# A D1 macaron layer on one core: attention probabilities turned in 32x32 squares by VectorE and a trip through DRAM

## The chip, the cores and the metric

One core of a Trainium2 chip. The metric is the device time of the core in microseconds; lower is better. The kernel before takes 1220.16 us, the median of 3 runs (1220.13 to 1220.35).

## The reference

```python
x = x + 0.5 * ffn(layernorm(x))          # x: 2 x 512 x 512 float32
x = x + attention(layernorm(x))
x = x + 0.5 * ffn(layernorm(x))
# attention, 32 query heads, 8 key/value heads of width 128, causal with an ALiBi bias:
scores = einsum('bkgqd,bksd->bkgqs', rmsnorm(q), rmsnorm(k)) / sqrt(128)
attn = softmax(scores + bias)            # bias is -1e30 above the diagonal
out = einsum('bkgqs,bksd->bkgqd', attn, v)
return out.reshape(b, s, 32 * 128) @ Wo.T
```

The feed-forward part is a gated linear unit whose weights are scaled by a product of rank 4. Everything is float32; TensorE works in a rounded format, so each operand is kept as a high part and a rest, and each product is made of three: high by high, high by low, low by high.

## The kernel before

The work is a first feed-forward pass, the attention, and a second feed-forward pass. The attention is cut in 64 **units**, `unit(n)` being one key/value head g with its 4 query heads, one batch and one block of 128 queries: n = 8 g + 4 b + t. A unit has t + 1 key blocks. Below, i is n modulo 4 (which is t) and "at" is n modulo 8.

Each engine has a program of its own, written out by hand as `slot(n)` for n = 0 to 63. Semaphores couple them; an engine takes its instructions strictly in order.

**TensorE** (`slot`, L707), in slot n: scores of unit n (for i = 0 in halves, L655 to L657, else L367 to L369 through `matmul3`); `weigh_values(n - 1)` (L677): for each key block the values' high part and rest times the high part of the turned probabilities (L688, L689), then the values' high part times their rest (L693); two of seven products that make queries, keys and values of the two units four slots ahead (`product_qkv`); `turn_rows(n + 1)`, whose results the next scores need (L619, L622); `project_out(n - 1)`, 12 products; one or two more products of the seven; and last `turn_probabilities(n)` (L666, instruction L674): for each key block, four 128x128 transposes against an identity into one PSUM bank.

**ScalarE** (`slot`, L1105): `exponentials(n)`, in between or behind them `weigh_values(n - 1)` (high part of the weighed values, L1086), `probabilities(n)` (L1075, times the inverse sum), takes of sums out of PSUM (`take_sum`, L1023), `turn_rows(n + 1)` (L1049, L1058), high parts of the next head group's weights (`split_qkv`, L977, instruction L988), `take_left` (L1030), and `turn_probabilities(n)`, the high part of each turned block (L1081).

**VectorE** (`slot`, L1602): `scores(n)` adds the bias and finds the top (L1517; at i = 0 L1504 and L1509), then sums of squares (L1466) and inverse roots in even slots, the inverse sum (L1522), `weigh_values(n - 1)` (rest, L1541), `add_products` (L1560), `turn_rows(n + 1)` (L1484, L1494), `project_out(n - 1)` (adds into a ring of two rows, L1550), and last `turn_probabilities(n)` (L1535): the rest of each turned block.

**GpSimd** (`slot`, L1819): squares of rows (L1811), norms (`norm_rows`, L1817), rests of the values, of the output weights (`split_o`) and of the group's weights (`split_qkv`), all through L1686, and `mix_qkv` (L1747, instruction L1761), which makes mixed weight blocks t1 to t4 out of b11, b12, b21 and b22. `QKV_WHEN` says in which slot of a group which block of the next group is split: b11 and b21 at 2, t2 and t1 at 3, t3, t4 and b22 at 4. Mixes t1 to t3 are made at 3, t4 at 4. The first products that use them are issued in slot at=4. A mixed block can be rounded by ScalarE only when GpSimd has made it:

```python
if block[0] == "t":
    act.wait_ge(qkv_mixed, QKV_MIXES.index((g, block)) + 1)
```

**SP** issues all transfers of this stretch from one queue: `load_qkv(g + 1)` at 1 and `load_o(g + 1)` at 6, both into the same room, so that each waits for the splits of the other; and for each unit `ring_store`, which waits for VectorE's add, and `ring_load`, which waits for the store to land.

Probabilities (`prob`), their turned parts (`probT_h`, `probT_l`) and the weighed values (`oT_h`, `oT_l`) have one room each. TensorE rotates over 7 PSUM banks in this stretch.

## Time and profile before

| | |
|---|---|
| median of 3 runs | 1220.16 us |
| the profiled execution, first to last instruction | 1218.6 us |
| TensorE busy | 1206.2 us, 99% |
| VectorE, ScalarE, GpSimd busy | 834.9, 753.5, 652.8 us |
| granted TensorE clock | 1.000 |
| turning of probabilities on TensorE | 640 instructions |
| DMA, mean | 77 GB/s |

Busy times of TensorE are of pipelined instructions whose ends are modelled: what one costs is the distance between starts.  A row of a stretch gives, behind its length, how long each engine was busy in it, with the number of instructions in brackets.

### The profile page before, as it was taken

The page shows a single profiled execution, that of the slowest core. Times are in us where ns is not written, and L with a number is a line of the kernel's source. Part 1 is how long each engine was busy: PE and PEld are TensorE (multiplying, and loading weights), DVE is VectorE, ACT ScalarE, POOL GpSimd, SP SyncE. Part 2 cuts the span into 40 slices and gives each one's busy share as a digit, 9 for nine tenths or more (in the row PEclk, how much of TensorE's full clock was granted, in tenths as well). Part 3 has the DMA queues.
Part 4 walks back from the last instruction along what each step waited for, and adds up shares of the span by engine and source line. Part 5 has one row for each costly group of instructions (what it writes and reads, how often), then busy time and mean ns, then how long its engine had stood idle before and what let it go on. Part 6 is the DMA issues. An engine that isn't in the chain of part 4 may idle for free.

```text
span 1218.6 us, 18533 instructions
## 1 busy us (share of the span) xinstructions
PE 1206.2 (99%) x6368; PEld 1062.1 (87%) x6368; DVE 834.9 (69%) x2035; ACT 753.5 (62%) x1758; POOL 652.8 (54%) x526
## 2 busy tenths in 40 slices
PE   6999999999999999999999999999999999999999
PEld 5888888899998999999999999999999888888887
DVE  7876665776666577677677677667767878755555
ACT  4554442357677767767768767767767774544442
POOL 5796561635675625724824824823824343865550
DMA  6152222212213123122122122122122020221101
GB/s 235 42 175 94 103 105 104 94 47 87 79 44 104 44 79 103 39 84 96 44 87 89 50 87 87 53 79 96 53 78 87 20 68 9 71 69 53 52 18 69
DMA packets 33596, 93.77 MB, mean 77 GB/s; under 512 B 4128, under 2 KB 5056, under 8 KB 31456
## 3 DMA queue, kind: packets, MB, share of 16 engines
q1 hardware_dynamic: 33264, 92.29, 22.2%
q8 instruction: 52, 0.85, 0.3%
q14 instruction: 40, 0.33, 0.1%
q10 hardware_dynamic: 240, 0.30, 0.1%
HBM read 62.69 MB, written 29.88 MB: 76 GB/s over the span
## 4 chain that ended last, share of the span: by engine, by line
PE 98%; DVE 1%; DMA 0%; ACT 0%; SPq 0%; issue 0%
PE bank L369 22%; PE bank L367 22%; PE bank L368 21%; PE bank L674 6%; PE bank L479 4%; PE bank L473 4%; PE bank L474 4%; PE bank L688 3%; PE bank L693 3%; PE bank L689 3%; PE bank L619 2%; PE bank L395 1%; PE bank L655 1%; PE bank L622 1%; PE bank L383 1%; DMA x_rows<-x 0%
## 5 line engine op out<-in xcount | busy, mean ns | idle before, releaser
L1066 ACT ACTIVATE prob<-prob,neg_top 128x128 f32<-128x128 f32 (+3 forms) x256 | 141.2, 554 | 87.6 <-DVE neg_top L1517 56.9
L1817 POOL TENSOR_TENSOR rows<-rows,row_root_y 128x640 f32<-128x640 f32 x64 | 80.5, 1257 | 194.1 <-DVE row_root_y L1205 192.9
L1811 POOL TENSOR_TENSOR square<-rows 128x640 f32<-128x640 f32 x64 | 79.3, 1254 | 158.7 <-DVE rows L1560 131.1
L1686 POOL TENSOR_TENSOR w_l_late<-raw_late,w_h_late 128x512 fp32r<-128x512 f32 (+1 forms) x59 | 91.5, 1565 | 71.8 <-ACT w_h_late L809 71.8
L1075 ACT ACTIVATE prob<-prob,inverse 128x128 f32<-128x128 f32 (+3 forms) x252 | 121.1, 553 | 4.4 <-DVE inverse L1522 4.4
L1535 DVE TENSOR_TENSOR probT_l<-bank,probT_h 128x512 fp32r<-128x512 f32 x160 | 101.4, 683 | 28.5 <-ACT probT_h L1081 28.5
L1081 ACT CAST probT_h<-bank 128x512 fp32r<-128x512 f32 x160 | 84.6, 596 | 41.4 <-PE bank L674 41.4
L1281 DVE SCALAR_TENSOR_TENSOR x_rows<-bank,x_rows 128x512 f32<-128x512 f32 x111 | 74.8, 687 | 44.4 <-PE bank L479 44.4
L367 PE MATMUL bank<-o_h,oT_h 128*128 128x512 f32 x256 | 104.7, 409 | 0.0
L369 PE MATMUL bank<-o_h,oT_l 128*128 128x512 f32 x256 | 100.8, 394 | 0.0
L368 PE MATMUL bank<-o_l,oT_h 128*128 128x512 f32 x256 | 99.8, 390 | 0.0
L1517 DVE CUSTOM_DVE_ANT_0 prob<-bank,bias 128x256 f32<-128x256 f32 (+3 forms) x200 | 97.0, 540 | 0.0
L1560 DVE TENSOR_TENSOR rows<-bank,rows 128x384 f32<-128x384 f32 x72 | 40.0, 555 | 79.2 <-ACT rows L1023 51.3
L674 PE MATMUL bank<-ident,prob 128*128 128x128 f32 x640 | 80.9, 273 | 0.3 <-ACT prob L1075 0.3
L674 PEld LDWEIGHTS bank<-ident,prob 128*128 128x128 f32 x640 | 73.8, 140 | 4.9 <-issue 0.9
L1686 POOL TENSOR_TENSOR w_l_early<-raw_early,w_h_early 128x512 fp32r<-128x512 f32 x37 | 48.6, 1328 | 41.5 <-ACT w_h_early L809 41.5
L367 PE MATMUL bank<-kT,qT_h 128*128 128x256 f32 (+3 forms) x192 | 67.7, 352 | 0.0
L841 ACT COPY part<-bank 128x512 f32<-128x512 f32 x66 | 38.5, 586 | 43.8 <-PE bank L369 43.4
L688 PE MATMUL bank<-probT_h,v_h 128*128 128x512 f32 x160 | 63.9, 399 | 0.1
L369 PE MATMUL bank<-kT,qT_l 128*128 128x256 f32 (+3 forms) x192 | 63.9, 333 | 0.0
L368 PE MATMUL bank<-kT,qT_h 128*128 128x256 f32 (+3 forms) x192 | 63.8, 332 | 0.0
L689 PE MATMUL bank<-probT_h,v_l 128*128 128x512 f32 x160 | 62.8, 392 | 0.0
(237 smaller groups left out, 3808.5 us busy)
## 6 DMA issues: line engine op xcount, KB each, us to landing
x_ring<-x_between SPq DMA_DIRECT2D x64, 256.0 KB, 2.6
x_between<-x_ring SPq DMA_DIRECT2D x56, 256.0 KB, 2.0
raw_late<-w_qkv SPq DMA_DIRECT2D x8, 1536.0 KB, 6.5
raw_early<-ffn_w SPq DMA_DIRECT2D x21, 512.0 KB, 4.1
scaled<-raw_early SPq DMA_DIRECT2D x21, 512.0 KB, 2.7
raw_late<-scaled SPq DMA_DIRECT2D x21, 512.0 KB, 3.7
raw_late<-w_o SPq DMA_DIRECT2D x8, 1024.0 KB, 5.0
x_between<-x_rows SPq DMA_DIRECT2D x8, 256.0 KB, 2.0
```

Of the source, the lines that this page charges most:

```text
L367: pe.matmul(bank, lh, rh, start=first, stop=False, skip_group_check=more)
L368: pe.matmul(bank, lh, rl, start=False, stop=False, skip_group_check=more)
L369: return pe.matmul(bank, ll, rh, start=False, stop=last, skip_group_check=more)
L674: last = pe.transpose(bank[:, h * P:(h + 1) * P], prob[:, h, j * P:(j + 1) * P], ident[:, :])
L688: pe.matmul(bank[:, :], v_h[:, b, j, :], turned[2 * j], start=j == 0, stop=False)
L689: pe.matmul(bank[:, :], v_l[:, b, j, :], turned[2 * j], start=False, stop=False)
L1066: last = act.activation(p, p, ACT.Exp, bias=neg_top[:, h:h + 1], scale=-1.0, accum_out=total[:, h:h + 1])
L1075: act.activation(p, p, ACT.Copy, scale=inverse[:, h:h + 1]).then_inc(prob_done, 1)
L1081: act.copy(probT_h[:, j, :, :], banks[r.bank][:, :].rearrange("p (h q) -> p h q", h=G)).then_inc(probT_hi_done, 1)
L1517: dve.tensor_tensor_reduce(prob[:, h, 0:keys], banks[r.bank][:, 0:keys], bias[:, h, S - keys:S], -(2.0 ** -g), -MASKED, ALU.add, ALU.min, ...
L1535: dve.tensor_tensor(probT_l[:, j, :, :], banks[r.bank][:, :].rearrange("p (h q) -> p h q", h=G), probT_h[:, j, :, :].bitcast(F32), ALU.sub ...
L1686: return pool.tensor_tensor(lo, raw, hi.bitcast(F32), ALU.subtract)
```

## The change

Units 12 to 52 (`BLOCKED`) are no longer turned by TensorE. VectorE transposes each 32x32 square of a key block in place of the whole (one instruction of 128x512 for a key block and four heads), into room that the activations no longer need. SP sends each such block to DRAM (256 KB, in pieces of 512 bytes), and fetches the unit back with four transfers, one for each 32 partitions, so that the squares come to lie where a full transpose would have them. The fetch lands in `probT_l`, and waits until the unit before has been weighed. ScalarE rounds the unit into `probT_h` with one instruction; VectorE makes the rest of the first half of the columns and GpSimd that of the second. The order of columns is (square row, head, query in the square), which the copies of the weighed values put right.

Such a unit is weighed and projected two slots after its scores and not one. The last of them, unit 52, is weighed in slot 53 behind the products. Because group ends are weighed later, in the groups g = 2 to 6 (`out_late`) output weights are split in slot at=1 behind the rest, the next group's weights are loaded in slot at=2, and blocks b11 and b21 are split in slot at=3, on GpSimd ahead of the mixes.

```diff
+SQ = 32
+SQS = P // SQ
+BLOCKED = range(12, UNITS - 11)
...
+        with ExitStack() as before:
+            squares_in = [sb(f"squares_in{n}", [KC, B * S], F32, before) for n in range(2)]
...
-                    {2: ("b11", "b21"), 3: ("t2", "t1"), 4: ("t3", "t4", "b22")})
+                    {2: ("b11", "b21"), 3: ("t2", "t1"), 4: ("t3", "t4", "b22")},
+                    {3: ("b11", "b21", "t2", "t1"), 4: ("t3", "t4", "b22")})
...
+        def weighed_in(n):
+            return [u for u in (n - 2, n - 1) if u >= 0 and u + (2 if u in BLOCKED[:-1] else 1) == n and u != BLOCKED[-1]]
+        def out_late(g):
+            return g * B * TB - 1 in BLOCKED
+        def qkv_when(g):
+            return QKV_WHEN[0 if g < SEVEN_FROM else 2 if out_late(g - 1) else 1]
+        def square_room(j):
+            free = squares_in[j // 2][:, j % 2, :].rearrange("p (u two c) -> p u two c", u=PAIRS, two=2)
+            return free[:, :, 1, :]
+        def turned(part, n):
+            return part[:, :, :, :].rearrange("p j h q -> p (j h q)")[:, 0:blocks(n) * G * P]
...
+                if n in BLOCKED:
+                    p_h, p_l = (turned(part, n).rearrange("p (a j c) -> p j a c", a=SQS, j=i + 1) for part in (probT_h, probT_l))
+                    pe.wait_ge(turned_hi, blocked_nth(n) + 1)
+                    for j in range(i + 1):
+                        pe.matmul(bank[:, :], v_h[:, b, j, :], p_h[:, j, :, :], start=j == 0, stop=False)
+                        pe.matmul(bank[:, :], v_l[:, b, j, :], p_h[:, j, :, :], start=False, stop=False)
+                    pe.wait_ge(turned_rest, blocked_nth(n) + 1)
+                    pe.wait_ge(turned_rest_pool, blocked_nth(n) + 1)
+                    for j in range(i + 1):
+                        last = pe.matmul(bank[:, :], v_h[:, b, j, :], p_l[:, j, :, :], start=False, stop=j == i)
+                    last.then_inc(full[r.bank], 1)
+                    return
...
-                if n:
-                    weigh_values(n - 1)
+                for u in weighed_in(n):
+                    weigh_values(u)
...
-                if n:
-                    project_out(n - 1)
+                for u in weighed_in(n):
+                    project_out(u)
...
-                turn_probabilities(n)
+                if n - 1 == BLOCKED[-1]:
+                    weigh_values(n - 1)
+                if n not in BLOCKED:
+                    turn_probabilities(n)
+                if n - 1 == BLOCKED[-1]:
+                    project_out(n - 1)
...
+            def round_turned(n):
+                act.wait_ge(prob_back, 16 * SQS * (blocked_nth(n) + 1))
+                act.copy(turned(probT_h, n), turned(probT_l, n).bitcast(F32)).then_inc(turned_hi, 1)
...
-                if n:
-                    weigh_values(n - 1)
+                for u in weighed_in(n):
+                    weigh_values(u)
...
-                splits = QKV_WHEN[g + 1 >= SEVEN_FROM].get(at, ()) if g < HKV - 1 else ()
+                splits = qkv_when(g + 1).get(at, ()) if g < HKV - 1 else ()
...
-                if at == 0:
+                if at == 0 and not out_late(g):
                     split_o(g, (0, 1))
                 if paired(ahead):
                     take_sum(ahead, 6) if n % 2 == 0 else take_left(ahead - 1)
-                if n:
+                if n - 1 in BLOCKED:
+                    round_turned(n - 1)
+                if n - 1 == BLOCKED[-1]:
+                    weigh_values(n - 1)
+                if n and n not in BLOCKED:
                     turn_probabilities(n)
-                if at == 0:
+                if at == 0 and not out_late(g):
                     split_o(g, (2, 3))
+                if at == 1 and out_late(g):
+                    split_o(g, range(G))
                 if behind:
                     split_qkv(g + 1, *splits)
...
+                if n - 1 in BLOCKED:
+                    dve.wait_ge(prob_blocked, blocks_until(n))
...
+            def block_probabilities(n):
+                if n == BLOCKED[0]:
+                    last = results["right", FIRST_PAIRED - 1]
+                    dve.wait_ge(full[last.bank], last.nth)
+                    dve.wait_ge(token_sums_done, 4 * PAIRS)
+                else:
+                    dve.wait_ge(prob_away, 16 * blocks_until(n))
+                dve.wait_ge(prob_done, sum(own_heads(u) for u in range(n + 1)))
+                for j in range(blocks(n)):
+                    squares = prob[:, :, j * P:(j + 1) * P].rearrange("p h (b k) -> p b h k", k=SQ)
+                    dve.transpose(square_room(j).rearrange("p b (h t) -> p b h t", t=SQ), squares).then_inc(prob_blocked, 1)
+            def turned_lo(n):
+                dve.wait_ge(turned_hi, blocked_nth(n) + 1)
+                half = blocks(n) * G * P // 2
+                rests = turned(probT_l, n)[:, 0:half]
+                dve.tensor_tensor(rests, rests.bitcast(F32), turned(probT_h, n)[:, 0:half].bitcast(F32), ALU.subtract).then_inc(turned_rest, 1)
...
+                if n in BLOCKED:
+                    dve.tensor_tensor(by_heads(oT_l), banks[r.bank][:, :].rearrange("p (a h t) -> p a h t", a=SQS, h=G),
+                                      by_heads(oT_h).bitcast(F32), ALU.subtract).then_inc(evac[r.bank], 1)
...
-                if n and not first:
-                    weigh_values(n - 1)
+                for u in () if first else weighed_in(n):
+                    weigh_values(u)
...
-                if n:
-                    project_out(n - 1)
+                for u in weighed_in(n):
+                    project_out(u)
                 if n == UNITS - 5:
                     output_statistics(UNITS - 6)
                 if paired(ahead) and n % 2:
                     add_products(ahead - 1, 3)
-                if n:
+                if n in BLOCKED:
+                    block_probabilities(n)
+                if n - 1 in BLOCKED:
+                    turned_lo(n - 1)
+                if n - 1 == BLOCKED[-1]:
+                    weigh_values(n - 1)
+                if n and n not in BLOCKED:
                     turn_probabilities(n)
+                if n - 1 == BLOCKED[-1]:
+                    project_out(n - 1)
...
+            def turned_lo(n):
+                pool.wait_ge(turned_hi, blocked_nth(n) + 1)
+                all_of_it = blocks(n) * G * P
+                rests = turned(probT_l, n)[:, all_of_it // 2:all_of_it]
+                rest(rests, rests.bitcast(F32), turned(probT_h, n)[:, all_of_it // 2:all_of_it]).then_inc(turned_rest_pool, 1)
...
-                if at == 1:
+                if at == 1 and not out_late(g):
...
+                splits = qkv_when(g + 1).get(at, ()) if g < HKV - 1 else ()
                 if at == 3:
+                    split_qkv(g + 1, *(block for block in splits if block[0] == "b"))
                     mix_qkv(g + 1, *mixes_now)
-                if g < HKV - 1:
-                    split_qkv(g + 1, *QKV_WHEN[g + 1 >= SEVEN_FROM].get(at, ()))
+                    split_qkv(g + 1, *(block for block in splits if block[0] == "t"))
+                else:
+                    split_qkv(g + 1, *splits)
                 if 0 <= n - LEAD - 1 < PAIRS:
                     token_sums_rest(n - LEAD - 1)
                 if 0 <= n - LEAD < PAIRS:
                     sum_tokens(n - LEAD)
+                if n - 1 in BLOCKED:
+                    turned_lo(n - 1)
+                if at == 1 and out_late(g):
+                    split_o(g, range(G))
...
+            def away(n):
+                return prob_turns[blocked_nth(n) % 2][:, 0:blocks(n) * G * P]
+            def send_probabilities(n):
+                nth = blocked_nth(n)
+                if nth > 1:
+                    sp.wait_ge(prob_back, 16 * SQS * (nth - 1))
+                for j in range(blocks(n)):
+                    sp.wait_ge(prob_blocked, blocks_until(n) + j + 1)
+                    rows_of = away(n).rearrange("p (b j c) -> p b j c", b=SQS, j=blocks(n))
+                    sp.dma_start(rows_of[:, :, j, :], square_room(j)).then_inc(prob_away, 16)
+            def fetch_turned(n):
+                sp.wait_ge(prob_away, 16 * blocks_until(n + 1))
+                before = results["values", n - 1]
+                sp.wait_ge(full[before.bank], before.nth)
+                for b in range(SQS):
+                    sp.dma_start(turned(probT_l, n)[b * SQ:(b + 1) * SQ, :].bitcast(F32).rearrange("k (a c) -> k a c", a=SQS),
+                                 away(n).rearrange("(a k) (b c) -> b k a c", a=SQS, b=SQS)[b]).then_inc(prob_back, 16)
...
-                if at == 1:
+                if n - 1 in BLOCKED:
+                    fetch_turned(n - 1)
+                if at == 1 + out_late(g):
...
-                if n:
-                    ring_store(n - 1)
-                if n and n + 1 < UNITS:
-                    ring_load(n + 1)
+                for u in [BLOCKED[-1]] * (n - 2 == BLOCKED[-1]) + weighed_in(n):
+                    ring_store(u)
+                    if u < UNITS - 2:
+                        ring_load(u + 2)
+                if n in BLOCKED:
+                    send_probabilities(n)
```

## Rows read from the trace of the kernel before

**Rows 1.** The page: busy time, share of the span, instructions.
```profile
PE 1206.2 (99%) x6368; PEld 1062.1 (87%) x6368; DVE 834.9 (69%) x2035; ACT 753.5 (62%) x1758; POOL 652.8 (54%) x526
```

**Rows 2.** Stretches: one slot each; length, busy by engine, clock, DMA share, GB/s.
```profile
636.46:647.06 10.60, 10.60 (x62) 9.50 (x61) 9.60 (x33) 6.99 (x24) 3.95 (x6) 1.00 0.08 25
...
657.56:668.81 11.25, 11.25 (x69) 10.40 (x67) 9.01 (x30) 9.91 (x25) 3.97 (x4) 1.00 0.14 48
668.81:682.88 14.07, 14.07 (x82) 12.64 (x80) 8.59 (x20) 10.93 (x24) 13.99 (x10) 1.00 0.17 58
```

**Rows 3.** Stretches from the first turning of probabilities to the slot's end, same columns.
```profile
646.71:647.06 0.35, 0.35 (x5) 0.35 (x4) 0.00 (x0) 0.35 (x2) 0.35 (x2) 1.00 0.00 0
...
681.21:682.88 1.67, 1.67 (x18) 1.67 (x16) 0.97 (x2) 1.03 (x3) 1.67 (x2) 1.00 0.24 91
sum 4.04, PE 4.04 PEld 4.03 DVE 2.72 ACT 2.77 POOL 3.25; mean PE 1.01 PEld 1.01 DVE 0.68 ACT 0.69 POOL 0.81
```

**Rows 4.** Stretches: scores at i=0, scores at i=1, twelve products weighing values; same columns.
```profile
682.88:683.83 0.95, 0.95 (x12) 0.95 (x10) 0.95 (x3) 0.95 (x3) 0.95 (x2) 1.00 0.55 149
693.48:694.99 1.51, 1.51 (x15) 1.51 (x14) 0.61 (x1) 0.87 (x2) 1.51 (x1) 1.00 0.49 176
683.83:686.64 2.81, 2.81 (x14) 2.31 (x14) 2.78 (x13) 0.52 (x4) 2.81 (x3) 1.00 0.11 43
```

**Rows 5.** Timeline of ScalarE, slot at=3: start us, us, instruction.
```profile
678.44 0.85 ACT L988 CAST w_h_late<-xn 128x768 fp32r<-128x768 f32 x1
...
680.37 0.48 ACT L1030 COPY rows<-bank 128x384 f32<-128x384 f32 x1 [0.34 <-PE bank L369]
```

**Rows 6.** Timeline of GpSimd, slots at=3 and at=4, same columns.
```profile
681.56 1.83 POOL L1686 TENSOR_TENSOR ahead_l<-xn,ahead_h 128x768 fp32r<-128x768 f32 x1
683.35 2.46 POOL L1811 TENSOR_TENSOR square<-rows 128x640 f32<-128x640 f32 x2
685.77 1.84 POOL L1761 TENSOR_TENSOR xn<-raw_late,xn 128x768 f32<-128x768 f32 x1
691.25 1.26 POOL L1817 TENSOR_TENSOR rows<-rows,row_root_y 128x640 f32<-128x640 f32 x1 [3.63 <-DVE row_root_y L1205]
692.46 0.88 POOL L1686 TENSOR_TENSOR v_l<-rows,v_h 128x128 fp32r<-128x128 f32 x2
```

**Rows 7.** GpSimd's rests: duration ns min/median/max, first and last start; shape.
```profile
L1686 POOL TENSOR_TENSOR sum_l<-sum,sum_h x4: 2381/2390/2402, 327.5 to 366.0; 128x1024 fp32r<-128x1024 f32 x4
```

**Rows 8.** VectorE's groups: line, names, shapes, count | busy us, mean ns | idle.
```profile
L1535 DVE TENSOR_TENSOR probT_l<-bank,probT_h 128x512 fp32r<-128x512 f32 x160 | 101.4, 683 | 28.5 <-ACT probT_h L1081 28.5
...
L1230 DVE TENSOR_SCALAR xn<-x_rows,mv,ln_root_y 128x512 f32<-128x512 f32 x20 | 9.6, 542 | 0.1
```

**Rows 9.** Timeline of VectorE, slots at=0 to at=3, columns as rows 5.
```profile
638.45 0.74 DVE L1504 TENSOR_TENSOR prob<-bank,bias 128x256 f32<-128x256 f32 x2
...
645.78 0.28 DVE L1494 TENSOR_TENSOR kT<-bank,kT 128x128 fp32r<-128x128 f32 x1
...
659.23 0.55 DVE L1517 CUSTOM_DVE_ANT_0 prob<-bank,bias 128x384 f32<-128x384 f32 x1
...
668.27 0.28 DVE L1494 TENSOR_TENSOR kT<-bank,kT 128x128 fp32r<-128x128 f32 x1
...
675.02 0.69 DVE L1541 TENSOR_TENSOR oT_l<-bank,oT_h 128x512 fp32r<-128x512 f32 x1 [0.29 <-ACT oT_h L1086]
```

**Rows 10.** The page: DMA issues by line, count, KB each, us to landing.
```profile
x_ring<-x_between SPq DMA_DIRECT2D x64, 256.0 KB, 2.6
x_between<-x_ring SPq DMA_DIRECT2D x56, 256.0 KB, 2.0
...
raw_late<-w_o SPq DMA_DIRECT2D x8, 1024.0 KB, 5.0
```

**Rows 11.** One line of VectorE, both operands in SBUF, columns as rows 7.
```profile
L1320 DVE TENSOR_TENSOR d_lo<-d,d_hi x44: 679/692/1772, 54.1 to 1207.6; 128x512 fp32r<-128x512 f32 x44
```

**Rows 12.** One line of TensorE, columns as rows 7.
```profile
L383 PE MATMUL bank<-fac_gu,fix x56: 277/283/581, 6.6 to 181.2; 128*128 128x256 f32 x56
```

36 lines of the change are left out of this document (26 added, 10 removed).

## The prediction

> **What bounds the kernel now.** I read the page first: TensorE is busy 1206.2 of 1218.6 us [rows 1], so time is saved only where TensorE has less to do, and lost wherever it waits. Then the stretches. The attention is 64 slots, and from slot 12 on four slots repeat without change; I write i for a slot's number modulo 4 and "at" for it modulo 8. The four last 10.60, 10.50 (from 647.06 to 657.56), 11.25 and 14.07 us with TensorE busy throughout and the granted clock at 1.00, the upper of its two levels, 2.4 GHz [rows 2]. So every other engine is today just early enough, and the question is by how much.
>
> **What goes.** The turning ends each slot and costs 0.35 us for one key block and 1.67 for four; the four slots together give 4.04 [rows 3]. Units 12 to 52 are ten such periods and one unit of one block: 10 x 4.04 + 0.35 = 40.8 us, 3.3% of the span. All of it is on the path.
>
> **What TensorE then has to do.** In slot n it makes the scores of n and weighs n-2. Scores take 0.95 us at i=0 and 1.51 at i=1; weighing four blocks takes 2.81 for 12 products, 0.234 each [rows 4], two thirds of them with the high parts. Slot lengths become 10.60 - 0.35 - 2.81 + 2.11 = 9.5 at i=0, 11.8 at i=1, 9.3 at i=2 and 11.75 at i=3, 42.4 in place of 46.4. The high part is first asked for in the next slot but one, right behind its scores.
>
> **The first cost: GpSimd in slots at=3 to 5.** With the change the next head group's weights are loaded one slot later, and the splits of blocks b11 and b21 move from at=2 into at=3, ahead of the mixes t1 to t3. ScalarE's copies of t2 and t1 wait for those mixes, and behind them on ScalarE stand take_left and the rounding of the unit turned last. Times from the start of slot at=3 (668.81 in rows 2), on which today ScalarE's first split copy starts at +9.63 and takes 0.85 [rows 5]; b11 takes that place, since what is ahead of it is unchanged. GpSimd then does, at 1.83 each [rows 6], the low parts of b11 and b21, the mixes t1, t2 and t3, the low parts of t2 and t1, and its half of the unit's low probabilities, 768 columns too: 10.5 + 8 x 1.83 = 25.1. ScalarE copies t2 from +17.8 and rounds the unit at about +21.4. TensorE wants the high part at 11.75 + 0.95 = 12.7 and, six products later, the low at 14.1. It waits 11.0. Next on GpSimd stand two squares 2.46, the mix t4 1.84, a norm 1.26, the value rests 0.88 [rows 6], three more low parts 5.5, and half of the four-block unit, 1024 columns, 2.39 [rows 7]: done at +39.4. TensorE, from 25.1, needs 0.7 + 6.5 + 1.5 + 1.9 to the same point, 35.7, and waits 3.7. That is 14.7 for each of the five groups in which slot at=3 has the late weights (slots 19, 27, 35, 43, 51): **73.5 us**. No price in it is unknown; only the place of b11 on ScalarE is carried over.
>
> **The second cost: VectorE's order.** Its turning of squares is in no row. Below it stands one pass over 512 SBUF columns, 542 ns, above it the two-operand rest, 683 [rows 8]; I take 0.6, since the turn has one operand but a broken order, and keep 0.54 and twice the upper row, 1.37, as ends. It replaces a rest of 0.683 by a turn of 0.6 and half a rest, about even in busy time. What changes is the order: turns and rest now stand between a slot's last work and the next scores.
> - i=2: VectorE needs 9.2 us from its scores (659.23) to the end of the keys' rest (668.27 + 0.28) [rows 9]. It gets to them at +2.1, behind two turns and a short rest; so the next slot's scores start at +11.3, where TensorE is through after 9.3. Wait 2.0.
> - i=3: the low part of the weighed values ends today 6.9 into the slot (675.02 + 0.69 [rows 9], slot from 668.81). VectorE starts such a slot 0.75 later, behind three turns and a rest, so 7.65; the projection would start 6.8 in (two stages of 12 products, 2.8 and 2.15, stand between it and the slot's end at 11.75). Wait 0.85.
> - i=0 (where GpSimd is not already later): four turns and a rest of 768 columns end at +0.56 + 2.4 + 0.9 = 3.9. The low part is due at 0.95 + 1.4 = 2.35, and the queue from scores (638.45) to the keys' rest (645.78 + 0.28) is 7.6 [rows 9], so the projection, through the same queue, starts late too: 2.3 in all.
> - i=1: ScalarE takes a sum as TensorE ends the slot before (as at 680.37, 0.48 [rows 5]), then rounds 2048 columns, 1.95 by the slope of its 768-column copy (an estimate): the high part is there at +2.45, due at +1.51; GpSimd's 2.39 adds 0.55. Wait 1.5.
> A plain period loses 6.65, the other kind 2.85 beside the first cost. Five of each: 33.3 + 14.3 = **47.6 us**. GpSimd's half of the rest costs nothing at i=2 and i=3: its queue is idle there, and it ends before VectorE's.
>
> **The road through DRAM** I cost at nothing, with its cover named. A unit's sends stand on SP behind a ring store, its landing (2.0) and a load; a ring load lands in 2.6 [rows 10], so a four-block unit is away 5.5 us into slot i=0, when its room (the unit before weighed) is free too. 1024 KB as one transfer lands in 5.0 [rows 10]; four transfers in a row at 2.6 each would be 10.4. With 5.0 the data is there at +10.5, while ScalarE comes to the rounding at about +12. Cover gone by 1.5 us, each further microsecond is lost.
>
> **The sum.** Against the profiled execution: 1218.6 - 40.8 + 73.5 + 47.6 = 1298.9; the median of the runs is 1220.16, 1.6 above that span, so **1300.5**.
>
> **A rule weighed.** VectorE's rest of two SBUF operands took 679 ns at best and 1772 at worst [rows 11], so something holds it up by as much as one GpSimd instruction. The Trainium skill, "SBUF — State Buffer", states that the port pair shared by the two is an exclusive lock. The changed kernel releases both halves of each rest by one event, and as rows show both prices, one behind the other makes i=1 longer by 1.2, five times: 1306.5 in place of 1300.5. The rule speaks against this change; I leave it in the range.
>
> **Rivals.**
> 1. **Faster: the gain stays whole.** Were the five group starts covered (ScalarE finding t2 mixed) and VectorE's turns near 0.35, TensorE would lose nothing: 1220.2 - 40.8 = 1179.4. It decides at 8.1 us of waits per head group, two periods' turning. For it speaks that all engines but TensorE are idle 30% or more; against it that GpSimd's seven instructions behind b11 are fixed in order. 0.10.
> 2. **GpSimd alone.** VectorE follows TensorE with its slack intact, the second cost falls away: 1220.2 - 40.8 + 73.5 = 1252.9. 0.17.
> 3. **The transport is late.** Pieces of 512 bytes to 32 partitions at a time land in 10.4 instead of 5.0: high part 3.8 later at five slots i=1, 1320. Nothing in the rows has such pieces. 0.13.
> 4. **A turn costs 1.37.** 0.77 more for each of nine turns that end before scores in a plain period, five in the others: 54 more, 1355. 0.06.
> 5. **The clock.** The first matmuls of the kernel, after 6.6 us of idleness, took up to 581 ns where the same shape has a median of 283 [rows 12]. If TensorE is so slowed behind each 8.7 us wait, a product stage of 2.1 takes twice as long, five to ten times: 1311 to 1321. The Trainium skill, "TensorE: Matmul & The Clock Gate", has the clock at 1.2 GHz after idleness; by it this happens behind the long waits. Part of it is hidden behind the wait for the low part. 0.12.
> The forecast itself, 1300.5 with its bounds (1280 to 1312), has 0.40; 0.02 is left for no change.
>
> **How the numbers follow.** Rivals 2 to 5 are all slower than before: slower by over 0.2% (what a measurement of this kernel can tell from no change, 2.4 us) is 0.88, faster 0.10, within 0.02. The range reaches from just below rival 2 to most of the way to rival 4: 1248 to 1345. It leaves out rivals 1 and 4 and no change.
>
> **What would show it.** Right, if the five long gaps of TensorE (8 to 12 us) stand in slots 20, 28, 36, 44 and 52 ahead of the weighing's products, released by ScalarE's copy into probT_h and then by GpSimd's rest; if ScalarE's copy of t2 has idled 6.5 us for the mix; if slots at=4 and 5 last about 20 and 15 us; and no L674 instruction is left between units 12 and 52 (404 fewer). A turn near 0.6. Plain slots at i=2 of 11.3, at i=0 of 11.8. Wrong, if slots at=4 stay under 12 us, if ScalarE's wait is for DMA (then rival 3), or if waits on VectorE at i=0 and 2 are missing (rival 2).

## The result, and the profile after

The changed kernel takes 1371.87 us (median of 4 runs, 1370.26 to 1374.65) against 1220.2 before: ratio 1.1245 [1.1229, 1.1261], 152 us slower. The forecast was 1300.5 with a range up to 1345: the direction came out, the size did not. Times are medians, and of the kernel below whose groups end on TensorE one run is left out that took 1976.5 us at a granted clock of 0.56.

Two parts of the page of the changed kernel, busy times and DMA issues (line numbers are those of the new kernel; `matmul3` is now L416 to L418):

```profile
span 1369.0 us, 18169 instructions
PE 1213.4 (89%) x5964; PEld 1041.4 (76%) x5964; DVE 888.5 (65%) x2076; ACT 752.0 (55%) x1698; POOL 732.4 (54%) x567
...
prob_turns<-squares_in SPq DMA_DIRECT2D x101, 256.0 KB, 3.4
...
probT_l<-prob_turns SPq DMA_DIRECT2D x40, 256.0 KB, 4.6
```

TensorE has 404 instructions fewer than in [rows 1], as foretold, and yet is busy 7 us longer and idle 156 us (12 before). Without the turning it would be busy 1206.2 - 40.8 = 1165.4 us; it is busy 48 us more than that. Some 33 of them are an estimate of what the lower clock takes (the granted clock is 0.964 on the mean where it was 1.000, all of the loss in slots 20 to 53); the rest is mostly the ends that the profile models ahead of each wait. Its wait lines, and those of the engines behind it:

```profile
ACT prob L1132 <- DVE neg_top L1599: 107.4, 47, 5.2
...
PE bank L738 <- ACT probT_h L1152: 63.7, 20, 8.4
...
ACT w_h_late L1054 <- POOL xn L1875: 33.3, 6, 6.6
...
PE bank L743 <- POOL probT_l L1800: 29.3, 15, 4.5
...
PE bank L416 <- DVE oT_l L1644: 24.5, 25, 1.4
...
DVE sums L1546 <- POOL square L1932: 23.1, 21, 3.1
...
PE bank L416 <- DVE qT_l L1564: 16.1, 10, 2.3
...
ACT probT_h L1152 <- DMA probT_l<-prob_turns: 11.3, 10, 1.8
```

(Waited in total us, times, longest.) The longest waits are the forecast's: TensorE for ScalarE's rounding and then for GpSimd's rest, ScalarE for GpSimd's mix (longest 6.6 us, five times). New to it are the waits for `qT_l`, VectorE's wait for GpSimd's squares, and the size of those for `oT_l`.

Eight slots of one group, n = 23 to 30, cut at the first scores product of each, so that they answer to [rows 2]:

```profile
557.30:570.86 13.56, 12.16 (x59) 10.37 (x60) 9.18 (x19) 8.21 (x19) 3.21 (x4) 1.00 0.56 156
570.86:584.07 13.21, 10.19 (x53) 8.57 (x53) 12.34 (x36) 5.99 (x19) 6.75 (x6) 1.00 0.64 181
584.07:601.84 17.77, 14.81 (x67) 12.74 (x66) 6.37 (x17) 8.70 (x20) 4.96 (x3) 0.81 0.31 80
601.84:614.96 13.12, 9.82 (x51) 8.37 (x51) 9.97 (x31) 10.27 (x25) 9.70 (x9) 1.00 0.57 179
614.96:628.50 13.54, 13.54 (x60) 11.62 (x61) 9.17 (x19) 8.43 (x18) 4.57 (x5) 0.87 0.57 188
628.50:651.24 22.74, 12.83 (x54) 10.82 (x54) 11.96 (x36) 10.63 (x25) 20.50 (x15) 0.70 0.48 128
651.24:669.52 18.28, 13.73 (x67) 11.98 (x66) 6.54 (x16) 8.60 (x20) 9.29 (x5) 0.91 0.21 64
669.52:681.33 11.81, 9.77 (x51) 8.39 (x51) 9.73 (x31) 7.61 (x21) 4.69 (x5) 1.00 0.67 199
sum 124.03, PE 96.84 PEld 82.86 DVE 75.26 ACT 68.44 POOL 63.68; mean PE 12.10 PEld 10.36 DVE 9.41 ACT 8.55 POOL 7.96
```

| slot | at=7 | 0 | 1 | 2 | 3 | 4 | 5 | 6 | sum |
|---|---|---|---|---|---|---|---|---|---|
| before | 14.07 | 10.60 | 10.50 | 11.25 | 14.07 | 10.60 | 10.50 | 11.25 | 92.84 |
| forecast | 12.6 | 11.8 | 13.3 | 11.3 | 12.6 | 20.6 | 15.5 | 11.3 | 109.0 |
| this group | 13.56 | 13.21 | 17.77 | 13.12 | 13.54 | 22.74 | 18.28 | 11.81 | 124.03 |
| median of the groups | 13.57 | 13.21 | 16.00 | 13.12 | 13.55 | 23.00 | 17.77 | 11.81 | 122.0 |

The shape is the forecast's, and every slot is longer than forecast: 13.0 us a group by the medians, 65 of the 71 us that were missed. So the cause is not one surprise at one place. How slot at=4 (from 628.50) begins, on ScalarE (start us, us, instruction, idle before it and its releaser), then on TensorE:

```profile
626.21 1.58 ACT L1054 CAST w_h_late<-raw_late 128x768 fp32r<-128x768 f32 x2
634.42 0.83 ACT L1054 CAST w_h_late<-xn 128x768 fp32r<-128x768 f32 x1 [6.64 <-POOL xn L1875]
...
636.27 1.47 ACT L1152 CAST probT_h<-probT_l 128x1536 fp32r<-128x1536 f32 x1
```

```profile
637.88 0.77 PE L738 MATMUL bank<-probT_h,v_h 128*128 128x512 f32 x1 [8.36 <-ACT probT_h L1152]
...
642.33 1.62 PE L743 MATMUL bank<-probT_l,v_h 128*128 128x512 f32 x3 [1.55 <-POOL probT_l L1800]
```

and on GpSimd:

```profile
637.88 2.55 POOL L1800 TENSOR_TENSOR ahead_l<-xn,ahead_h 128x768 fp32r<-128x768 f32 x1
640.38 1.81 POOL L1800 TENSOR_TENSOR probT_l<-probT_l,probT_h 128x768 fp32r<-128x768 f32 x1
```

The order is the forecast's, the places are not quite. From the start of slot at=3 (614.96) the copy of b11 starts at +11.25 in place of +9.63 (626.21), that of t2 at +19.5 in place of +17.8, the high part is there at +22.8 in place of +21.4, and the low part at +27.2 in place of +25.1: 1.6 us from b11, and 0.7 from GpSimd's last rest for the weights, which took 2.55 us and not 1.83 (the others a little less). TensorE's wait is 8.36 us where 21.4 - 12.7 = 8.7 was foretold, but by luck: TensorE asks 1.8 us later too, since slot at=3 lasts 13.54 us and not the 11.75 of its own work.

### The profile page after: what moved, and what is told of

Same layout as the page of the kernel before. It is cut to its first block, busy times and chain, and to the rows that moved or that the text cites. A ratio compares the mean times of both kernels' runs of the same rounds, so it can differ in the third digit from the quotient of the medians.

```text
span 1369.0 us, 18169 instructions
## 1 busy us (share of the span) xinstructions
PE 1213.4 (89%) x5964; PEld 1041.4 (76%) x5964; DVE 888.5 (65%) x2076; ACT 752.0 (55%) x1698; POOL 732.4 (54%) x567
## 4 chain that ended last, share of the span: by engine, by line
PE 61%; POOL 14%; DVE 10%; ACT 7%; DMA 4%; issue 3%; SPq 1%; DVEq 0%; POOLq 0%; ACTq 0%
PE bank L416 14%; PE bank L418 14%; PE bank L417 13%; PE bank L528 4%; PE bank L523 4%; PE bank L522 4%; ACT prob L1132 3%; POOL probT_l L1800 3%; DVE squares_in L1631 3%; POOL ahead_l L1800 3%; POOL w_l_late L1800 2%; DMA probT_l<-prob_turns 2%; POOL square L1932 2%; PE bank L723 2%; DMA prob_turns<-squares_in 2%
## 5 line engine op out<-in xcount | busy, mean ns | idle before, releaser
L1800 POOL TENSOR_TENSOR probT_l<-probT_l,probT_h 128x256 fp32r<-128x256 f32 (+3 forms) x41 | 71.4, 1741 | 167.4 <-ACT probT_h L1152 167.4
L416 PE MATMUL bank<-o_h,oT_h 128*128 128x512 f32 x256 | 105.2, 411 | 24.5 <-DVE oT_l L1644 24.5
L1932 POOL TENSOR_TENSOR square<-rows 128x640 f32<-128x640 f32 x64 | 83.8, 1326 | 55.8 <-DVE rows L1666 28.2
L738 PE MATMUL bank<-probT_h,v_h 128*128 128x512 f32 x101 | 46.8, 463 | 63.9 <-ACT probT_h L1152 63.7
L418 PE MATMUL bank<-o_h,oT_l 128*128 128x512 f32 x256 | 100.5, 393 | 0.0
L1638 DVE TENSOR_TENSOR probT_l<-probT_l,probT_h 128x256 fp32r<-128x256 f32 (+3 forms) x41 | 53.7, 1309 | 54.7 <-ACT probT_h L1152 54.7
L416 PE MATMUL bank<-kT,qT_h 128*128 128x256 f32 (+3 forms) x192 | 66.8, 348 | 16.1 <-DVE qT_l L1564 16.1
L416 PEld LDWEIGHTS bank<-o_h,oT_h 128*128 128x128 f32 x256 | 48.1, 188 | 39.1 <-DVE oT_l L1644 30.9
L738 PEld LDWEIGHTS bank<-probT_h,v_h 128*128 128x128 f32 x101 | 21.9, 217 | 70.9 <-issue 67.0
L743 PE MATMUL bank<-probT_l,v_h 128*128 128x512 f32 x101 | 39.1, 491 | 36.0 <-POOL probT_l L1800 29.3
L1546 DVE TENSOR_REDUCE sums<-square 128x5 f32<-128x640 f32 x64 | 51.3, 816 | 23.1 <-POOL square L1932 23.1
L418 PE MATMUL bank<-kT,qT_l 128*128 128x256 f32 (+3 forms) x192 | 65.1, 339 | 0.0
```

The lines of the kernel that those rows point to most:

```text
L416: pe.matmul(bank, lh, rh, start=first, stop=False, skip_group_check=more)
L418: return pe.matmul(bank, ll, rh, start=False, stop=last, skip_group_check=more)
L738: pe.matmul(bank[:, :], v_h[:, b, j, :], p_h[:, j, :, :], start=j == 0, stop=False)
L1800: return pool.tensor_tensor(lo, raw, hi.bitcast(F32), ALU.subtract)
L1932: pool.tensor_tensor(square[:, n % 2, :, :], row, row, ALU.mult).then_inc(squares_done, 1)
```

## The experiments

All ratios are to the kernel before on the same chip. Slot lengths are medians over n = 12 to 53, cut as above.

**Late weights alone.** The kernel before, with nothing turned elsewhere; only loads, splits and GpSimd's order are the change's, in the five groups.

```diff
-    {2: ("b11", "b21"), 3: ("t2", "t1"), 4: ("t3", "t4", "b22")})
+    {2: ("b11", "b21"), 3: ("t2", "t1"), 4: ("t3", "t4", "b22")},
+    {3: ("b11", "b21", "t2", "t1"), 4: ("t3", "t4", "b22")})
...
-                if at == 1:
+                if at == 1 + out_late(g):
                     if g < HKV - 1:
                         load_qkv(g + 1)
```

> The kernel before, with TensorE turning everything, and of the change only the weights' part: in groups 2 to 6 the next group's weights are loaded in slot at=2, b11 and b21 split in slot at=3, on GpSimd ahead of the mixes. If the order on ScalarE and GpSimd is what the first cost says, ScalarE's copy of t2 waits 6.6 us for the mix five times, the unit's own casts come 5 to 6 us late, and the kernel takes 25 to 45 us more than before: 1245 to 1265. If the long waits need the squares' road (later rounding, more work on GpSimd), it stays within 8 us of 1220.

1259.82 us, ratio 1.0323 [1.0293, 1.0353]: 39.7 us, as the order on ScalarE and GpSimd had it. ScalarE's copy of b11 starts here at +9.64, its place in the kernel before, and that of t2 waits 6.64 us. The slot at=4 of one group, in it the stage that weighs the values (twelve products), and the products behind it:

```profile
598.67:617.33 18.66, 13.41 (x62) 11.55 (x61) 10.38 (x33) 11.36 (x29) 16.42 (x13) 0.82 0.05 14
605.04:610.29 5.25, 5.25 (x12) 4.10 (x13) 4.83 (x16) 2.95 (x11) 5.25 (x5) 0.50 0.00 0
610.29:612.60 2.31, 2.31 (x13) 2.27 (x12) 2.18 (x7) 2.04 (x7) 1.70 (x1) 0.91 0.00 0
```

The wait is 5.3 us; and behind it the granted clock is 0.50 (1.2 GHz) and twelve products take 5.25 us where [rows 4] show 2.81. So 2.4 to 2.7 of the 8.1 us of this group are the lower clock. Over the five groups TensorE is busy 1.5 to 3.0 us longer in this slot, 11 us in all: here rival 5 of the prediction is real.

**Filling the wait.** The kernel after, with 35 products whose results are overwritten ahead of the wait in slots at=4.

```diff
+                    for _ in range(35 if n % 8 == 2 and n > 16 else 0):
+                        pe.matmul(bank[:, :], v_h[:, b, 0, :], v_h[:, b, 0:4, :].rearrange("p t c -> p (t c)"), start=True, stop=True)
                     pe.wait_ge(turned_hi, blocked_nth(n) + 1)
```

> The change, with 35 products of 512 columns (about 8.1 us) put on TensorE in slots 20, 28, 36, 44 and 52 between the scores and the wait for the turned probabilities; their results are overwritten. They fill the 8.4 us in which TensorE waits. If the low granted clock behind these waits costs time, the products behind them come back to full speed (weighing and the products of slot at=4 shrink by 2.5 to 4 us) and the kernel takes 12 to 20 us less: 1352 to 1360. If only the wait itself costs, 1370 to 1374.

1372.76 us (1368.9 to 1376.7), ratio 1.1248: nothing gained. The granted clock of the same slot is 0.93 in place of 0.70, but in the weighing the wait for GpSimd's half of the rest is 2.94 us in place of 1.55: there the slow products had run beside GpSimd's rest. And the low clock moved: in four of the five groups it now falls in slot at=0 (0.78), which lasts 15.2 to 15.4 us, against a median of 13.2 in the kernel after. One of them:

```profile
573.74:589.11 15.37, 12.44 (x54) 10.64 (x53) 11.72 (x36) 6.59 (x19) 7.13 (x6) 0.78 0.72 189
```

The mean clock of the kernel is 0.973 against 0.964. So the run shows that this wait is not worth filling, but not what the low clock costs in the full change.

**No road through DRAM.** Sends, fetches and their waits are left out, so the probabilities weighed are not those of the unit.

```diff
-                act.wait_ge(prob_back, 16 * SQS * (blocked_nth(n) + 1))
...
-                    dve.wait_ge(prob_away, 16 * blocks_until(n))
...
-                    fetch_turned(n - 1)
...
-                    send_probabilities(n)
```

> The change without its transfers: nothing is sent to DRAM or fetched, and nobody waits for it; ScalarE rounds what lies in the room. All other instructions and their order stay. ScalarE waited for the fetch 11.3 us in all, so if the engines' order makes the result, it takes 5 to 20 us less than 1371.9: 1352 to 1367. If the road through DRAM sets the pace (rival 3), it falls below 1320.

1366.05 us, ratio 1.1193 [1.1161, 1.1226]: the road costs 6 us, half of the 11.3 us that ScalarE waits for it. Slots at=1, the place that rival 3 named, fall from 16.0 to 14.6 us.

**No road, short turns.** As before, and each of VectorE's turns is of 32 columns.

```diff
-                    dve.transpose(square_room(j).rearrange("p b (h t) -> p b h t", t=SQ), squares).then_inc(prob_blocked, 1)
+                    dve.transpose(square_room(j)[:, 0, 0:SQ], prob[:, 0, j * P:j * P + SQ]).then_inc(prob_blocked, 1)
```

> No transfers (as in the kernel without the road, 1366 us), and each of VectorE's 101 turns cut to one block of 32 columns, so that VectorE's turning costs next to nothing: the probabilities weighed are not the turned ones. The 101 turns are 0.62 us each from start to start, 63 us of VectorE's time in all. Theory: in the plain slots (n mod 8 = 6, 7, 0, 1, 2) the turning in the middle of VectorE's slot is on the path and sets some 35 to 55 us: 1311 to 1331 us, and the waits of products for VectorE's half of the rest shrink. Rival: GpSimd's queue (rests, squares) sets those slots too, and VectorE's time is only cover: 1350 to 1366 us.

1338.85 us, ratio 1.0969 [1.0905, 1.1032]: 27 us less, between the two expectations. TensorE's waits for `oT_l` fall from 19.2 us (24.5 with the road) to 3.7, the slots at=6, 7 and 0 shorten by 1.1, 1.9 and 2.1 us; at=1, 2 and 3 stay within 0.3, so there something else was as late. This shows whose waits they were: the low part of the values waits for ScalarE's exponentials, these for VectorE's maxima, and these for the turns.

**VectorE's order.** The rest of n-1 ahead of the turning of n.

```diff
-                if n in BLOCKED:
-                    block_probabilities(n)
                 if n - 1 in BLOCKED:
                     turned_lo(n - 1)
+                if n in BLOCKED:
+                    block_probabilities(n)
```

> The kernel after with two of VectorE's steps exchanged: its half of the rest of unit n-1 ahead of the turning of unit n. Theory (VectorE's order costs): the rest comes earlier by the length of the turns (0.6 to 2.5 us) in slots in which products wait for it (n mod 8 = 0 and 6 above all), 10 to 30 us in all: 1342 to 1362 us. Rival (the rest waits for ScalarE's rounding anyway, and VectorE now waits in front of its turns, so the squares are sent later, too late in slots with a short cover): 1372 to 1400 us, with new waits of the rounding for the transfers.

1383.67 us, ratio 1.1336: 12 us slower, on the rival's side. TensorE's wait for `probT_h` at L738 grows from 63.7 to 77.7 us, and ScalarE's for the fetches from 11.3 to 25.9: VectorE stands in front of its turns, and the squares are sent later.

**Values taken early.** ScalarE rounds the values behind the first head's exponentials, VectorE takes the rest ahead of the inverted sums.

```diff
-                soon = G // 2 if unit(n)[2] == 1 else G
+                soon = 1 if n - 2 in BLOCKED and n - 1 != BLOCKED[-1] else G // 2 if unit(n)[2] == 1 else G
...
-                first = unit(n)[2] == 1
+                first = unit(n)[2] == 1 or n - 2 in BLOCKED
```

> The kernel after, with the values of unit n-2 taken up early: ScalarE rounds them behind the first head's exponentials instead of the second's or the last's, VectorE takes their rest ahead of the inverted sums in every slot. In the kernel after the output projection waits 1.1 to 1.4 us for oT_l in the slots n mod 8 = 2, 3, 6 and 7, and 0.5 in 0. Theory (these waits set the plain slots): they go, 15 to 30 us in all: 1342 to 1357 us. Rival (ScalarE's exponentials, now later by the rounding of the values, set the turning and the next scores, so the time comes back): 1362 to 1385 us.

1387.36 us, ratio 1.1365: 15.5 us slower, just above the rival's range. The waits for `oT_l` are gone, and TensorE's for `probT_h` are 75.9 and for `qT_l` 23.0 (63.7 and 16.1 before the edit). So a wait seen in the trace was not a term of the sum: the rival's reading is that the exponentials, pushed later, set what follows.

**The whole rest on VectorE**, for all units, and then only for units n mod 8 = 3 and 4 (with `n % 8 in (3, 4)` in place of `True`). The first lines are TensorE's, the next VectorE's, the last GpSimd's.

```diff
-                    pe.wait_ge(turned_rest_pool, blocked_nth(n) + 1)
+                    if not (True):
+                        pe.wait_ge(turned_rest_pool, sum(not (True) for u in BLOCKED if u <= n))
...
-                half = blocks(n) * G * P // 2
+                half = blocks(n) * G * P // (1 if True else 2)
...
             def turned_lo(n):
+                if True:
+                    return
                 pool.wait_ge(turned_hi, blocked_nth(n) + 1)
```

> The kernel after with the whole rest of the turned probabilities on VectorE, none on GpSimd: GpSimd loses 42 subtractions of 0.9 to 3.6 us, VectorE's grow from half to the whole (0.38, 0.6, 0.9, 1.2 us more). Theory (GpSimd's queue and the two engines' slowing each other cost more than VectorE's added time): 1345 to 1367 us, slots with n mod 8 = 5 lose their wait for GpSimd (3 to 4.5 us). Rival (VectorE is the bound of the plain slots, so every added piece is paid): 1380 to 1410 us.

> As the one before, but the whole rest is VectorE's only for the units with n mod 8 = 3 and 4, whose rests stand behind the weights' splits and mixes in GpSimd's queue; the other 32 units keep both halves. Theory (GpSimd's queue): slots n mod 8 = 4 and 5 lose their waits for GpSimd's half, 1.6 and 3.0 us in each of five groups, less 0.5 to 1.2 us of VectorE's: 1350 to 1364 us. Rival (VectorE's rest ends no earlier than GpSimd's did, or what follows waits for GpSimd anyway): 1366 to 1375 us.

1339.19 us, ratio 1.0971 [1.094, 1.1003], and 1352.02, ratio 1.1077 [1.1018, 1.1135]: 32.7 and 19.9 us less, the first more than either theory gave, the second as the first theory had it. Of the 6.8 us a group that the first saves by the medians, 1.3 fall in slots at=1, 2.4 in at=4 and 2.9 in at=5. The rests by shape, in the kernel after (halves on two engines; count | busy us, mean ns | idle):

```profile
L1638 DVE TENSOR_TENSOR probT_l<-probT_l,probT_h 128x1024 fp32r<-128x1024 f32 x10 | 18.3, 1828 | 24.5 <-ACT probT_h L1152 24.5
L1638 DVE TENSOR_TENSOR probT_l<-probT_l,probT_h 128x512 fp32r<-128x512 f32 x10 | 15.4, 1536 | 0.0
L1638 DVE TENSOR_TENSOR probT_l<-probT_l,probT_h 128x768 fp32r<-128x768 f32 x10 | 14.3, 1431 | 30.2 <-ACT probT_h L1152 30.2
...
L1800 POOL TENSOR_TENSOR probT_l<-probT_l,probT_h 128x1024 fp32r<-128x1024 f32 x10 | 31.8, 3175 | 16.8 <-ACT probT_h L1152 16.8
```

and with the whole on VectorE:

```profile
L1639 DVE TENSOR_TENSOR probT_l<-probT_l,probT_h 128x2048 fp32r<-128x2048 f32 x10 | 29.6, 2956 | 24.9 <-ACT probT_h L1153 24.9
L1639 DVE TENSOR_TENSOR probT_l<-probT_l,probT_h 128x1536 fp32r<-128x1536 f32 x10 | 17.8, 1779 | 30.9 <-ACT probT_h L1153 30.9
L1639 DVE TENSOR_TENSOR probT_l<-probT_l,probT_h 128x1024 fp32r<-128x1024 f32 x10 | 11.8, 1181 | 0.0
```

VectorE does 1024 columns alone in 1181 ns, and 512 of them beside GpSimd in 1536: here the half takes longer than the whole. (For four key blocks it does not, 1828 against 2956 ns; there GpSimd's half, 3175, is the late one.) How, is seen on the two engines' timelines in the kernel after, first GpSimd, then VectorE:

```profile
615.67 1.29 POOL L1800 TENSOR_TENSOR probT_l<-probT_l,probT_h 128x512 fp32r<-128x512 f32 x1
616.90 1.26 POOL L1938 TENSOR_TENSOR rows<-rows,row_root_y 128x640 f32<-128x640 f32 x1
```

```profile
615.38 1.88 DVE L1631 STREAM_TRANSPOSE squares_in<-prob 128x512 f32<-128x512 f32 x3
617.19 1.52 DVE L1638 TENSOR_TENSOR probT_l<-probT_l,probT_h 128x512 fp32r<-128x512 f32 x1
```

VectorE's rest starts 0.29 behind GpSimd's norm, which ends at 618.16, and ends itself 0.55 later. The turn, which has one operand, takes 0.62 beside GpSimd's rest, as elsewhere. In the plain slots at=1 the two halves start together, and then it is GpSimd's that takes longer:

```profile
588.50 1.23 DVE L1638 TENSOR_TENSOR probT_l<-probT_l,probT_h 128x1024 fp32r<-128x1024 f32 x1 [3.73 <-ACT probT_h L1152]
```

```profile
588.55 3.41 POOL L1800 TENSOR_TENSOR probT_l<-probT_l,probT_h 128x1024 fp32r<-128x1024 f32 x1 [4.14 <-ACT probT_h L1152]
```

GpSimd's half takes 3.41 us there and 2.33 where no instruction of VectorE lies beside it (656.99): 1.08 more, about the length of VectorE's. The Trainium skill, "SBUF — State Buffer", section "Who interferes with whom", has a VectorE instruction with two SBUF inputs contend with a GpSimd instruction that reads SBUF, and the one issued second wait for the whole of the other; the trace agrees in both places (VectorE 1.52 us where half of 1181 ns would do, GpSimd 3.41 where 2.33 would).

**Groups that end on TensorE.** The last unit of each group is turned by TensorE and its values weighed with the ones before it, in one slot; then no weights have to wait. Alone, and with the whole rest on VectorE.

```diff
-BLOCKED = range(12, UNITS - 11)
+BLOCKED = [n for n in range(12, UNITS - 11) if n % 8 != 7]
+ENDS = {n for n in BLOCKED if n + 1 not in BLOCKED}
...
```

> The change, but the last unit of each head group (units 15, 23, 31, 39, 47) is turned by TensorE and weighed one slot later as before, so that no weights move: loads and splits stand where they stood. 36 units are turned in squares. First cost gone: slots at=4 fall from 23 to about 13 us, at=5 from 17.5 to 16, 11 to 12 us a group, less 1.7 for the turning that comes back and 1 to 2 for the joint: 1371.9 - 5 x 9 = 1327, between 1310 and 1340. If the transport or VectorE's order alone made the result, it stays above 1350; if the weights were all of it, it falls below 1240.

> Two edits together: the last unit of each group is turned by TensorE (so the weights' loads and splits stay where they were in the kernel before; alone it gave 1341.5 us) and the whole rest is VectorE's (alone 1339.2, 32.7 us under the kernel after). Theory (the two costs lie in different slots and mostly add): 1305 to 1328 us, since the slots n mod 8 = 4 have no long wait left from which VectorE's part gained. Rival (GpSimd's part in the joint slots n mod 8 = 5 and 7 was what the first edit left over): 1285 to 1304 us. If both edits remove the same waits: 1332 to 1342 us.

1341.47 us (one run; the expected range ended at 1340) and 1301.19 (two runs, 1296.53 and 1305.84), ratio 1.0659 [1.0614, 1.0704]: the second on the rival's side. Slots at=4 fall from 23.0 to 13.0 us, but the joint slots at=7 last 23.5. The two edits give 30.4 and 32.7 alone and 70.7 together, more than their sum: in the first kernel TensorE waits for GpSimd's half 2.3 us at at=3 (the slot lasts 15.7, then 13.4) and 2.5 to 4.4 at at=5 (20.2, then 13.8). At at=5 the clock takes part too: TensorE is busy 15.2 us at a clock of 0.83, then 12.2 at 1.00.

**Single units in squares.** Only n = 19, 27, 35, 43, 51; then all odd n from 13 to 51 with n mod 8 = 1, 3 or 5. Each is weighed at the end of the very next slot, with the whole rest on VectorE.

```diff
-BLOCKED = range(12, UNITS - 11)
+BLOCKED = [n for n in range(12, UNITS - 11) if n % 8 == 3]
...
-            return [u for u in (n - 2, n - 1) if u >= 0 and u + (2 if u in BLOCKED[:-1] else 1) == n and u != BLOCKED[-1]]
+            return [u for u in (n - 2, n - 1) if u >= 0 and u + 1 == n and u not in BLOCKED]
...
```

> Squares for the units n = 19, 27, 35, 43 and 51 alone (n mod 8 = 3), each turned by VectorE through DRAM, with the whole rest on VectorE, and weighed at the end of the next slot, ahead of that slot's own turning; everything else as in the kernel before. TensorE loses five turnings of 1.67 us, 8.4 us in all. Theory (what costs in the kernel after is the rounding, the rest and the turns on engines that are full when every unit has them and the weights' splits wait too; alone, a unit's fit into the slot): 1212 to 1220 us. Rival (even alone, VectorE's 2.5 us of turning and 1.5 us or more of rest delay the scores' maxima or the rows of the same slot by as much as TensorE saves): 1221 to 1240 us.

> As the one before, with squares for every unit from 13 to 51 with n mod 8 = 1, 3 or 5, no two of them next to each other. TensorE loses some 19 us of turning. Theory as before (alone in its two slots, a unit's squares fit): 1203 to 1222 us. Rival (VectorE and ScalarE are late in the slots n mod 8 = 2, 4, 6 where the rest and the values now stand): 1226 to 1270 us, with waits of the products for the rest at the ends of those slots.

1287.46 us, ratio 1.0546 [1.0531, 1.0562], and 1365.87, ratio 1.1184: far off both expectations, 13.4 us lost for each of five units. One of them, slot by slot (n = 27, 28, 29), then its sends on SP, and lines of ScalarE and of TensorE:

```profile
590.83:603.23 12.40, 12.40 (x65) 11.01 (x64) 7.63 (x18) 9.89 (x21) 12.32 (x9) 1.00 0.15 51
603.23:628.74 25.51, 14.68 (x60) 11.99 (x60) 13.15 (x35) 9.97 (x24) 17.03 (x12) 0.73 0.37 99
628.74:639.15 10.41, 10.41 (x66) 9.72 (x64) 5.64 (x16) 6.01 (x18) 0.00 (x0) 1.00 0.23 76
```

```profile
604.70 2.79 SPq L2147 DMA_DIRECT2D prob_turns<-squares_in  x4
```

```profile
607.82 0.40 ACT L1133 ACTIVATE prob<-prob,neg_top 128x128 f32<-128x128 f32 x1 [4.95 <-DVE neg_top L1592]
...
617.05 1.90 ACT L1153 CAST probT_h<-probT_l 128x2048 fp32r<-128x2048 f32 x1 [1.92 <-DMA probT_l<-prob_turns]
```

```profile
611.57 0.66 PE L416 MATMUL bank<-w_h_late,sum_h 128*128 128x384 f32 x1 [4.59 <-ACT rows L1090]
...
619.10 0.77 PE L738 MATMUL bank<-probT_h,v_h 128*128 128x512 f32 x1 [5.27 <-ACT probT_h L1153]
```

From the first send (604.70) to the rounding (617.05) are 12.35 us, more than a slot, and the next exponentials have idled 4.95 us for VectorE's four turns. Slot 27 gains 1.67 us and slot 28 loses 14.9. TensorE waits 4.6 us for rows that stand behind the late exponentials on ScalarE and 5.3 for the rounding, of which 1.9 is ScalarE's own wait for the fetch, and weighs at the lower clock (0.73 over the slot). So with one slot of depth even one unit in eight costs, and the fetch accounts directly for only 1.9 of the 14.9 us. That depth alone would cure it is not shown: no run changes only the depth.

**What is left when the parts are gone.** First, the whole rest on VectorE, no road, short turns; then the same with groups that end on TensorE; then also VectorE's rest cut to 32 columns (the edit below). (The results are not those of the units, as above.)

```diff
+                half = SQ
                 rests = turned(probT_l, n)[:, 0:half]
```

> The whole rest on VectorE (alone 1339.2), no transfers, and VectorE's turns cut to one block of 32 columns each (these two alone 1338.9): rounding, rest, late weights and the values two slots behind are left of the change. The kernel after is 1371.9, so the one edit gave 32.7 and the other 33.0. Theory (turns and rest are separate terms of the sum): 1298 to 1314 us. Rival (both edits empty the same slots' waits): 1318 to 1335 us. Rival on the other side (VectorE's queue is one chain, and a wait that both shorten goes wholly): 1275 to 1296 us.

> The same two edits on the kernel whose groups end on TensorE, with the whole rest on VectorE (1301.2): of the change, rounding, rest and the values two slots behind are left, for 36 units. Theory (turns and road cost 33.0 for 41 units, so 29 for 36): 1264 to 1280 us, still over the kernel before, since the joint slots n mod 8 = 7 wait for the rounding of two units. Rival (turns and road are what makes the joint slots long): 1225 to 1258 us.

> As the one before, and VectorE's rest cut to 32 columns for each unit: 36 subtractions of 0.6 to 3.0 us gone. What is left of the change is ScalarE's rounding in one piece and the order on TensorE. Theory (VectorE's queue ahead of the next scores sets the slots): 15 to 35 us under the kernel with the rest, 1235 to 1260 us. Rival (the rest lies beside other work by now): within 10 us of it, 1262 to 1280 us. If even this is above 1220 us, the order itself (values two slots behind, two units weighed in one slot) costs, not the work added to VectorE.

1304.87, 1274.95 and 1236.86 us, ratios 1.0694 [1.0663, 1.0725], 1.0449 [1.0398, 1.05] and 1.0137 [1.0107, 1.0166]. All three lie where the first theory put them (the last step, 38 us, slightly over its 15 to 35). Together they make a staircase:

| kernel | us | step | granted clock |
|---|---|---|---|
| after | 1371.9 | | 0.964 |
| the rest in one piece on VectorE | 1339.2 | -32.7 | 0.977 |
| and no road, short turns | 1304.9 | -34.3 | 0.975 |
| and no late weights (36 units) | 1275.0 | -29.9 | 0.989 |
| and hardly a rest | 1236.9 | -38.1 | 0.997 |
| before | 1220.2 | | 1.000 |

Each step removes waits, and with them some of the low clock; what a part costs by its wait and what by the clock behind it, the steps do not tell apart. The two runs of a rung lie up to 5 us from each other.

The last step is not a cost of the change alone: the kernel before does the same subtraction, 683 ns for each block [rows 8], but a block at a time beside TensorE's next turning. Done as one piece behind one rounding, in front of the next maxima, it is on the path. And with nothing left but ScalarE's rounding, short turns and rests, and values weighed two slots behind, the kernel is still 16.7 us slower than before.

## Why the prediction was right or wrong

- **What goes** (40.8 us): TensorE's instructions went, 404 of them, but as time they can't be separated: the last kernel above keeps this gain for 36 units (40.8 - 5 x 1.67 = 32.4 us) and still loses. The step took the turning as "all of it is on the path". On TensorE it was; that the chain of maxima, exponentials and values behind it was hardly shorter is how we read the last kernel, and not measured by itself.
- **The first cost** (73.5 us): order as foretold, ScalarE's idle time for t2 6.6 us where 6.5 was said, but all of it 1.6 us late. "b11 takes that place, since what is ahead of it is unchanged" failed: ahead of it on ScalarE stand the exponentials, which wait for VectorE's maxima, and those now stand behind three turns and a rest. ScalarE's first exponential starts 4.40 us into the slot (619.36), against 2.78 in the kernel with late weights alone, where b11 kept its place. Nor do GpSimd's instructions behind it follow each other without a gap: the norm waits 2.2 us for VectorE's inverse roots (648.57; [rows 6] show such a wait, of 3.63), and one rest takes 2.82 us in place of 1.85, so its 1024 columns are done at +44.4 and not at +39.4. Late weights alone cost 39.7. Slots at=4 and 5 last 23.0 and 17.8 us against forecasts of 20.6 and 15.5; that they last 20.65 and 14.8 with the whole rest on VectorE, which is not the kernel that was priced, confirms nothing.
- **The rest in two halves**: this is the largest step that failed. The prediction put VectorE's part as "about even in busy time" and GpSimd's as costing nothing at i=2 and 3, and took 2.39 us for 1024 columns from [rows 7], where it stands in another stage. Measured: 3175 ns on the mean, 3.41 us beside VectorE's half, and at two key blocks VectorE's half (1536 ns) slower than the whole (1181). The split costs 32.7 us. The rule weighed there pointed the right way, and was sized at 6: it was applied to five slots i=1, one half behind the other. The slots at=4 and 5 gain most when the split goes, and VectorE's halves wait for other instructions of GpSimd too, norms and weights' rests.
- **The second cost** (47.6 us; its own terms add up to 47.5): mechanism right, list too short. A turn costs 0.62 from start to start, against 0.6 taken. But the waits were worked out one slot at a time, each engine's queue starting on time. Turns and road give back 33 to 34 us; the other waits, `qT_l` at the start of slots at=3 among them (2.2 us, five times), come on top. About half of that one has its cause on GpSimd, in a part that no step costed, the output weights' rests moved behind the turned rest and ahead of the squares:

```profile
602.07 0.75 POOL L1800 TENSOR_TENSOR probT_l<-probT_l,probT_h 128x256 fp32r<-128x256 f32 x1 [8.90 <-ACT probT_h L1152]
602.77 5.23 POOL L1800 TENSOR_TENSOR o_l<-raw_late,o_h 128x512 fp32r<-128x512 f32 x4
607.95 2.48 POOL L1932 TENSOR_TENSOR square<-rows 128x640 f32<-128x640 f32 x2
```

```profile
609.25 0.82 DVE L1546 TENSOR_REDUCE sums<-square 128x5 f32<-128x640 f32 x1 [0.68 <-POOL square L1932]
...
613.92 0.74 DVE L1564 SCALAR_TENSOR_TENSOR qT_l<-bank,q_scale,qT_h 128x512 fp32r<-128x512 f32 x1
```

  In the kernels whose groups end on TensorE, and these rests stay where they were, that wait is 1.0 us, so 1.2 of 2.2.
- **The road** (nothing, cover of 1.5 us): 6 us, mostly in slots at=1. Four fetches land 4.6 us each and overlap, so rival 3 (20 us) was too dark.
- **The clock** (rival 5, 11 to 21 us, left out of the sum): real where weights alone are late, 11 us of 39.7. In the full change TensorE's own work takes some 33 us longer by the estimate above, and part of that is hidden and part not. Hidden: slots at=3 last 13.54 to 13.56 us at a clock of 0.87 and of 1.00 alike. Not hidden: in three groups slot at=5 had a clock of 0.90 or 0.91 and at=4 and 5 lasted 41.0 to 41.1 us together; in the fourth it had 1.00 and they lasted 39.6.
- **What stays open**: how much of the 71 us missed is the lower clock; what of them lies in VectorE's queue beyond the split (with the whole rest on VectorE the kernel is still 38.7 us over the forecast); how the 16.7 us of the last kernel divide between the rounding in one piece and two units weighed in one slot; and a version with squares that beats the kernel before was not found.

## What to carry to other kernels

Here several engines ended a slot together, and 40.8 us taken from the busiest bought nothing: in such a kernel price the chain (maxima, exponentials, values, projection) and not the busy time; and where a queue gets new work at its end, ask what the next slot's first instruction on that queue is. Where a sum carries a start over from the kernel before, ask what that engine waits for ahead of it. Splitting one subtraction of two SBUF operands between VectorE and GpSimd can be slower than leaving it whole. Compare the way of what comes back through DRAM with the depth in slots: here 12.35 us against slots of 10.5 to 14; with two slots the road cost 6 us, with one ScalarE still waited 1.9 us for it.
